# x, context and weights stored with the contraction on partitions: a transformer layer on one core without input transposes

## The reference

```python
# x, ctx: (16, 256, 512); Wq, Wk, Wv, Wo: (512, 512); W_fc: (2048, 512); W_proj: (512, 2048); all float32
def attn(x):                       # attention over HEADS within one token, 32 x 32 scores each
    q = split_qk(x @ Wq.T) * 16 ** -0.5          # (b, n, 32, 16)
    k = split_qk(x @ Wk.T); v = (x @ Wv.T)       # v: (b, 16, n, 32)
    att = softmax(nan_to_num(einsum('bnqd,bnkd->bnqk', q, k)))
    lam = exp(sum(lq1 * lk1)) - exp(sum(lq2 * lk2)) + LAM_INIT
    diff = att[:, :, :16, :16] - lam * att[:, :, 16:, 16:]
    out = einsum('bnah,bhnd->bnad', diff, v)
    out = out * rsqrt(mean(out * out, -1) + 1e-5) * (1 - LAM_INIT)
    return out.reshape(b, n, 512) @ Wo.T + bo
def xattn(q, c):                   # r = decay * r + c * c along the sequence
    return q * scan(c * c, decay)
def ternary(w):                    # groups of 64 along the last axis, in bfloat16
    scale = clip(mean(abs(wg)), 1e-8); return clip(round(wg / scale), -1, 1) * scale
def ffn(x):
    h = square(relu(x @ ternary(W_fc).T))
    return rms_norm(h) @ ternary(W_proj).T
x = layernorm(x + attn(x)); x = layernorm(x + xattn(x, ctx)); x = layernorm(x + ffn(x))
```

## Time and profile before

| | |
|---|---|
| median of 3 runs | 1272.43 us (1271.53 to 1276.82) |
| profiled execution | 1274.55 us, of which the span from first to last instruction is 1272.7 us |
| busy PE, DVE, ACT, POOL | 1100.6, 939.4, 587.1, 205.9 us |
| chain that ended last | PE 66%, DVE 9%, ACT 7%, issue 7%, SP's queue 5%, DMA 4% |
| phase A, from the first projection to the end of P11 of superblock 7 | 26.17 to 514.6 us |
| between the phases, to the regular feed-forward bodies | 514.6 to about 664 us |
| phase B | some 81.6 us for each superblock |

### The profile page before, as it was taken

How to read it: one execution, slowest core, us unless ns; L and a number is a source line. 1 busy time by engine, 2 the same in 40 slices (tenths; PEclk the granted TensorE clock), 3 DMA queues, 4 the chain that set the end, 5 groups by cost and what they waited for, 6 DMA issues and landing times.

```text
span 1272.7 us, 22077 instructions
## 1 busy us (share of the span) xinstructions
PE 1100.6 (86%) x7424; PEld 873.7 (69%) x7424; DVE 939.4 (74%) x1932; ACT 587.1 (46%) x906; POOL 205.9 (16%) x202
## 2 busy tenths in 40 slices
PE   5988989889797979635599998998989989899995
PEld 4766767667575757424378787787877878778784
DVE  4287878787878888786858677696785867958746
ACT  4333333333243333310346555566555655655683
POOL 3100030303131312132140103003030030210000
PEclk9999999999898989767599999999999999999998
DMA  7566475766657565983530021201211012100001
GB/s 278 158 175 160 140 163 174 157 186 137 200 120 221 100 183 117 290 215 113 193 100 34 1 67 67 66 10 56 66 66 53 13 66 66 66 1 2 34 1 66
DMA packets 184334, 139.32 MB, mean 109 GB/s; under 512 B 140128, under 2 KB 152416, under 8 KB 180192
## 3 DMA queue, kind: packets, MB, share of 16 engines
q1 hardware_dynamic: 113120, 113.57, 31.8%
q10 hardware_dynamic: 71168, 25.17, 8.2%
HBM read 82.09 MB, written 52.43 MB: 106 GB/s over the span
## 4 chain that ended last, share of the span: by engine, by line
PE 66%; DVE 9%; ACT 7%; issue 7%; SPq 5%; DMA 4%; POOL 1%; ACTq 0%; DVEq 0%; POOLq 0%
PE ps_f L558 18%; PE ps_s L744 14%; PE ps_f L728 12%; PE ps_s L577 9%; PE ps_o L679 6%; DMA qbd<-q_scr 3%; SPq L382 3%; PE ps_o L597 2%; ACT h_sb L947 2%; DVE h_acc L1279 1%; ACT r_sb L941 1%; PE ps_t L619 1%; PE ps_f L679 1%; DMA w_raw<-in_L_attn_Wv 1%; ACT oth L919 1%
## 5 line engine op out<-in xcount | busy, mean ns | idle before, releaser
L728 PE MATMUL ps_f<-x2h,w 128*128 128x512 f32 x512 | 204.7, 400 | 1.6 <-DVE x2l L1260 1.6
L744 PE MATMUL ps_s<-w,hh 128*128 128x512 f32 x500 | 201.5, 403 | 0.0
L728 PE MATMUL ps_f<-x2l,w 128*128 128x512 f32 x512 | 200.7, 392 | 0.0
L744 PE MATMUL ps_s<-w,hl 128*128 128x512 f32 x500 | 199.3, 399 | 0.0
L1268 DVE TENSOR_TENSOR hl<-h_sb,hh 128x512 fp32r<-128x512 f32 x128 | 91.1, 712 | 112.2 <-ACT hh L951 110.5
L577 PE MATMUL ps_s<-qbd,k 128*32 128x128 f32 x2048 | 125.4, 412 | 55.0 <-DMA qbd<-q_scr 55.0
L558 PE MATMUL ps_f<-xth,wh 128*128 128x512 f32 x384 | 157.0, 409 | 1.6 <-DVE xtl L1044 1.6
L558 PE MATMUL ps_f<-xth,wl 128*128 128x512 f32 x384 | 150.3, 391 | 0.0
L558 PE MATMUL ps_f<-xtl,wh 128*128 128x512 f32 x384 | 149.8, 390 | 0.0
L577 PEld LDWEIGHTS ps_s<-qbd,k 128*32 128x32 f32 x2048 | 83.4, 149 | 91.9 <-issue 48.7
L1453 POOL TENSOR_TENSOR xb<-xb,bob 128x512 f32<-128x512 f32 x32 | 71.8, 2274 | 434.9 <-DMA xb<-in_x 434.9
(11 more groups left out here) (142 smaller groups left out, 1918.8 us busy)
## 6 DMA issues: line engine op xcount, KB each, us to landing
xa<-in_x SPq DMA_DIRECT2D x8, 1024.0 KB, 5.4
q_scr<-f_sb ACTq DMA_DIRECT2D x32, 256.0 KB, 2.6
k_scr<-f_sb ACTq DMA_DIRECT2D x32, 256.0 KB, 2.8
v_scr<-f_sb ACTq DMA_DIRECT2D x32, 256.0 KB, 5.7
k<-k_scr SPq DMA_DIRECT2D x8, 1024.0 KB, 7.5
qbd<-q_scr SPq DMA_DIRECT2D x128, 64.0 KB, 4.8
w_scr<-w_st SPq DMA_DIRECT2D x32, 256.0 KB, 4.9
v<-v_scr SPq DMA_DIRECT2D x64, 128.0 KB, 6.0
```

The source lines that it names most:

```text
L728: last = nc.tensor.matmul(ps_f[:, j % 2, :], w1[:, k, j * P:(j + 1) * P], xx[:, k, :], start=(k == 0 and xx is x2h), stop=(k == KC - 1 and ...
L744: last = nc.tensor.matmul(ps_s[:, t, :], a[:, j % 4, t * P:(t + 1) * P], w2[:, j, :], start=(j == 0 and a is hh), stop=(j == HC - 1 and a ...
```

## The change

The host now stores x, the context and all weights so that the contraction stands on partitions (`layouts`), and x is passed twice, turned for the projections and as before for the residual. So these fall away: the 64 transposes of the start, `x_transpose`, `w_transpose`, `w_copy` with `w_st`, and `ctx_transpose`. ACT and DVE split x and the four square weights from SBUF, not from PSUM. x is double-buffered: `x_upper(i + 1)` and `x_lower(i + 1)` run inside body i. With groups of 64 now across partitions, the group sums are matmuls with a block matrix of ones (`w_sums`, 4 in a body), and `w_signs` is two operations for each half; POOL makes two products for each half in `w_in`, 8 in a body, and SP writes `w_in` itself, and reads the next piece into it when that write has landed. The scores, mixes, exponentials and loads have new places; `wo_scr` is written at the end of body 0; the loop holds two bodies.

```diff
-        W_FIRST = (8, 9)
-        W_SECOND = 1
+        AT_SCORES = (0, 1, 6, 8)
+        AT_MIX = (3, 4, 5, 6)
+        AT_SUMS = (4, 5, 10, 10)
...
 def phase_a(eng, body):
-            with eng.Fori(2, NSB) as i:
-                body(i, True, True)
+            with eng.Fori(1, NSB // 2 - 1) as h:
+                body(h * 2, 0, True, True)
+                body(h * 2 + 1, 1, True, True)
+            body(NSB - 2, 0, True, True)
+            body(NSB - 1, 1, True, True)
...
 # SP
             def first_half_load(i):
-                hold((s_ps, at(i, 16, 0)) if later(i) else (zeroed, 2), *f_written(i, (0, 1, 5, 6, 7)))
+                hold(*([(s_ps, at(i, 16, 0))] if later(i) else [(zeroed, 2), (wo_wr, 32)]),
+                     *f_written(i, (0, 1, 5, 6, 7)))
...
+            def w_load(i, u):
+                if u:
+                    hold((wt_wr, at(i, 32, 16)))
+                    sp.dma_start(w_in[:].rearrange("p (r d) -> p r d", d=D), proj_in[i]).then_inc(wt_ld, 16)
+                    return
+                if later(i):
+                    hold((wt_wr, at(i, 32, 0)))
+                sp.dma_start(w_in[:].rearrange("p (k n) -> p k n", k=KC), fc_in[i]).then_inc(wt_ld, 16)
+            def w_write(i, u):
+                hold((wt_qs, at(i, 4, 2 * u + 2)))
+                sp.dma_start((w1_scr, w2_scr)[u][i], w_in[:]).then_inc(wt_wr, 16)
...
+            def body(i, par, do_2, do_1):
+                if later(i) and not (isinstance(i, int) and i == NSB - 1):
+                    x_load(i + 1, 1 - par)
                 if do_2:
                     dbd_load(i - 2)
+                if later(i):
+                    w_write(i - 1, 1)
+                    w_load(i, 0)
                 if do_1:
                     second_half_load(i - 1)
                 if do_1:
                     v2_load(i - 1)
+                w_write(i, 0)
+                w_load(i, 1)
+                if not later(i):
+                    wo_write()
                 first_half_load(i)
...
             dbd_load(NSB - 2)
+            second_half_load(NSB - 1)
             hold((f_ps, at(NSB, 12, 0)), (wo_wr, 32), (o_wr, 16))
             load_first(0)
...
-            second_half_load(NSB - 1)
...
 # PE
+            def w_sums(i, u, r):
+                pe.wait_ge(wt_b, at(i, 2, u + 1))
+                ...
+                nc.tensor.matmul(sums_bank(u, r), blk[:], w_b[:, half(r)], start=True, stop=True).then_inc(wt_ps, 1)
+            def body(i, par, do_2, do_1):
                 for n in range(12):
+                    project(i, n, par)
+                    if do_2 and n in AT_MIX:
+                        mix(i - 2, AT_MIX.index(n), 0, G // 4)
+                    if do_1 and n in AT_SCORES:
+                        scores(i - 1, AT_SCORES.index(n), 0, FULL)
+                    for u, r in itertools.product(range(2), range(2)):
+                        if n == AT_SUMS[2 * u + r]:
+                            w_sums(i, u, r)
...
 # ACT
+            def body(i, par, do_2, do_1):
                 for n in range(12):
                     f_copy(i, n)
+                    if do_1 and n in (1, 3, 8, 11):
+                        exps(i - 1, (1, 3, 8, 11).index(n))
+                    if n == 2:
+                        w_abs(i, 0)
+                        w_sign(i, 0)
+                    if do_2 and n in (4, 5, 6):
+                        mixed(i - 2, n - 4)
+                    if do_2 and n == 6:
+                        mixed(i - 2, 3)
+                    if n == 7 and not (isinstance(i, int) and i == NSB - 1):
+                        for k in range(KC):
+                            x_upper(i + 1, 1 - par, k)
...
 # DVE
+            def w_signs(i, u, r):
+                ...
+                nc.vector.tensor_scalar(gscale[:, half(r)], sums_bank(u, r), 1.0 / WGROUP, 1e-8, ALU.mult,
+                                        ALU.max).then_inc(wt_gs, 1)
+                v.wait_ge(wt_gs, at(i, 4, done))
+                nc.vector.scalar_tensor_tensor(out=w_b[:, half(r)], in0=gscale[:, half(r)], scalar=257.0 / 512.0,
+                                               in1=w_b[:, half(r)], op0=ALU.mult, op1=ALU.is_lt).then_inc(wt_pn, 1)
```

More of the change, by code:

```diff
@@ L563, in project @@
-                    beside(k)
+                last.then_inc(f_ps, 1)
             def scores(i, c, first, end):
@@ L970, in _ @@
             exps(NSB - 1, 2)
+            for k in range(KC):
+                ctx_square(0, k)
             mixed(NSB - 2, 2)
             mixed(NSB - 2, 3)
+            out_upper(0)
             exps(NSB - 1, 3)
@@ L1164, in body @@
                     mixed_turn(i - 2, 1)
+                    square_sum(i - 2, 0)
+                w_signs(i, 0, 0)
                 if do_1:
@@ L1168, in body @@
                     mixed_turn(i - 2, 2)
[L1169 to L1170 removed]
+                    square_sum(i - 2, 1)
+                w_signs(i, 0, 1)
+                if not later(i):
+                    for k in range(KC):
+                        w_lower(3, k)
                 if do_2:
[L1172 removed]
                     mixed_turn(i - 2, 3)
                     square_sum(i - 2, 2)
[L1175 to L1177 removed]
                     square_sum(i - 2, 3)
@@ L1180, in body @@
                 if do_1:
+                    soft_first(i - 1, 2)
                     soft_second(i - 1, 2)
+                if not (isinstance(i, int) and i == NSB - 1):
+                    for k in range(KC):
+                        x_lower(i + 1, 1 - par, k)
+                if do_1:
                     soft_first(i - 1, 3)
+                w_signs(i, 1, 0)
+                if do_1:
                     soft_second(i - 1, 3)
                     diff_turn(i - 1)
-                w_signs(i, 1)
+                w_signs(i, 1, 1)
+                if not later(i):
+                    lam_make()
             phase_a(v, body)
```

519 lines of the change are left out of this document (199 added, 320 removed).

## The result

The changed kernel takes 1191.86 us (median of 4 runs, 1186.81 to 1196.98) against 1272.65 us before: a ratio of 0.936, with a 95% interval from 0.9313 to 0.9406. A second measurement, made with the last experiments, gave 1193.36 us and 0.935 (0.9334 to 0.9365). 1188 was forecast, within 1162 to 1216. The profiled execution is the slowest of its four (1196.98 us, span 1195.2), so stage by stage it shows 77.5 us less than the profile of before, where the medians differ by 81.

What follows compares the result with a forecast made beforehand. It took `w_in`'s circle to bound phase A at 59 us a body and PE to bound phase B. Gains of 62 up to superblock 7, 6 between the phases and 16 in phase B made 84, so 1272.43 became 1188, within 1162 to 1216.

Steps and rivals of the forecast that it cites:

- The circle: Phase A: `w_in`'s write, reload and use through SP, ACT and DVE back to `diff_turn` sets the body, 58.5 us.
- the waits by which it would show on PE: Phase A, bodies 2 to 7: PE's waits would be ended by ACT's `f_copy` 3 and not by `qbd`.
- Start: Start to first `soft_first`: S0 at 53.3, `soft_first` at 57.2 instead of 72.47, 15.3 us earlier, between 11 and 19.
- 6 us for issue and landing: Start: time for Wo's two writes to be issued and land before `first_half_load(0)` may go, leading to 42.5 us.
- half a meeting: Phase A: POOL's eight products would lengthen two-input DVE operations by 0.5 us a body, between 0 and 7.4.
- PE's floor binds: Rival, phase A: `w_in` lands faster, ACT is never late, a body is 56.5 us, total 1173; chance 0.17.
- my own case: Main case: phase A bodies of 58 to 61 us, other terms near their values, total 1172 to 1205; chance 0.58.
- Both things by which I would have called myself wrong: Phase A: PE's waits staying on `qbd`, or DVE rows with two inputs longer than before the change.
- Between the phases: Superblock 7's first `soft_first` to the end of `out_lower(0)`: 6 us of 58.1 gained, between 0 and 10.
- Phase B: Context transposes gone: 2.5 us in each of six full bodies, 15, plus 1 in body 0; bounds 0 and 20.
- POOL and DVE do collide: Rival, phase A: six of eight POOL products meet DVE, 5 us a body more, total 1221; chance 0.12.
- The slow rival: Phase A: four serial `w_in` transfers a body decide; at 5 us longer each, total 1308; chance 0.03.

Runs made afterwards that it cites:

- e3: Changed kernel with Wo's high part in the raw Wq's place, so the first `k2` load no longer waits for Wo's writes: 1192.2 us, ratio 0.9345.
- e1: Changed kernel with the write of `w_in`'s second half and the load of its next first half on ACT's queue instead of SP's: 1190.4 us, ratio 0.9333.
- e2: Changed kernel with the load of `w_in`'s first half put behind the second half of the q load in SP's queue: 1222.3 us, ratio 0.9596.
- e7: Changed kernel with one more DVE reduction of 1024 columns per body, ahead of the first square's reduction: 1197.6 us, ratio 0.9375.
- e10: Changed kernel writing back only 16 of 1024 columns of `w_in`'s second half in bodies 1 to 7, leaving out work: 1189.2 us, ratio 0.9311.
- e6: Changed kernel with superblock 7's second half of `qbd` loaded behind the context, `ot` and Wo, as before the change: 1205.1 us, ratio 0.945.
- e12: Changed kernel with e3's start and half the DMAs of `dbd` and of `qbd`'s first half issued by ACT: 1185.4 us, ratio 0.9296.
- e13: e12 with the four `x_lower` ahead of `soft_second` 2 and POOL's first two products held until they are done: 1184.2 us, ratio 0.9284.

## Why the forecast was right, point by point

The total is right partly by luck: the start gained 4 us less than forecast and phase B 6 less in this profile, and bodies 2 to 7 of phase A gained 6 more. The circle that it named is what the experiments bear out; the waits by which it would show on PE were wrong.

**Start.** P0 starts at 9.56 (forecast 10.5), and the last write of Wo goes out at 37.19 (36.5). Its landing is the mis-sized term: 6 us for issue and landing, taken from a write a quarter of the size, were 8.7. From `k2`'s issue to S0 it was 11.0 (10.8). The 2 us for a cold start of PE stand in the trace: the first eleven matmuls are some 0.43 us apart, and 0.23 from 14.3 us on, where the granted clock is 1.00. So 11.4 us were gained and not 15.3, and with the usual start of 63 only 9.5, below the 11 that I had given as the least. e3 shows that this landing was what stood there.

**Phase A.** The circle was named rightly and e1, e2, e7 and e10 bear it out; a body took 58.0 us for 59, and superblock 7 stands at 462.0 for 463. Inside, two errors cancel. From the end of `diff_turn` it is 13.2 us to the start of `w_abs`, not 15.8: `dbd` took 5.25, and 4.9 us was no low price for this write of 512 KB but a high one, 3.5 in the row above (the other write of a body, of the same size, takes 6.8 to 8.2 and is not on the circle). ACT took 6.3 (6). DVE needed 38.5 us from the first square's sum to the end of `diff_turn`, not 36.7: POOL lengthens four of its rows there by 2.2 us, where I had allowed half a meeting, 0.5 (last section). And the `x_upper`, which I had put at nothing because ACT waits for PE there, stand ahead of `exps` 2 on the chain: they and `f_copy` 8 hold it back by up to 0.9 us.

**PE.** Its floor is 54.4 us and not 56.5. I had worked it from a body of before in which the granted clock was 0.96; in the body above it is 1.00, and PE waits for less. The rival "PE's floor binds" could not have happened at 56.5, and what I named as the sign of my own case, PE's waits ended by `f_copy` 3, was wrong: they are ended by DVE's mix copies and `qbd`. `f_copy` 3 becomes PE's wait only when the circle is 3 us longer (e2). Both things by which I would have called myself wrong came true in part: 7.1 of PE's 21.6 us of waiting stayed on `qbd`, and DVE rows with two inputs are longer than before. That `w_in` binds all the same is what e1, e2, e7 and e10 show, not the waits.

Nor did ACT's waits for `w_in` need to reach PE: they reach DVE through the square. `w_abs` waited 3.39 us for `w_in`, as said (3 or more).

**New operations.** The `w_signs` pairs took 0.65 to 0.69 us an operation and `x_lower` 0.69: as forecast.

**Between the phases.** 7.0 for 6, but as the difference of larger terms than I had: 11 for the moved half of `qbd` (e6), less 4 for the rest. Behind it 2.2 us were lost that I had not counted: the squares share one buffer, so the second `square_sum` there waits 1.19 us, and the first two projections together took 0.9 us more than before, since the granted clock, 0.50 at their start in both kernels, rose 1.8 us later after the change.

**Phase B.** 9.8 us for 16 in this profile. The work taken away is as priced, 2.5 us a body (the last full body, at a granted clock of 1.00 in both kernels, went from 77.8 to 75.4); but the clock took part of it back (next section).

**Rivals.** POOL and DVE do collide, as the Trainium skill says (SBUF — State Buffer, "SBUF: two separate sides"), at 2.2 us on the circle in a body, over the 0.5 allowed, and not at 5. The slow rival was far off: the two transfers of `w_in` on the circle took 3.5 and 3.8 us, no more than the 4.9 and 3.8 of the earlier trace rows. It was right in one thing, that each us in them is a us of the body (e2).

## What to carry to other kernels

Here the chain closed through a wait of about 1 us in each turn, and the other rings were about 1 us behind it: lengthening the ring cost nearly one for one, and shortening it paid only down to the next. Shortening it alone by 1.5 gained 1.3 us a body (e10), two rings together 1.0 (e12), three 1.1 (e13). So look at how long DVE's or PE's wait in the ring is before you shorten it: that is about all there is to gain. Work out an engine's floor from a body without waits and at full clock, not from busy time. And ask of work that is taken away whether it stood in a wait that will now be one long gap.
